# Two weight copies of a mixture-of-experts stage as a maximum, and three row-address steps moved up

## The reference

```python
x = x + xattn(norm(x), ctx, ctx, Wq, Wk, Wv, Wo, bo, mask)   # 16 heads of 64, causal
n = norm(x)
z = norm(n) * ln_g + ln_b
probs = softmax(z @ rW + rb)                                 # 8 experts
w = the two largest of probs, scaled to sum 1
hid[e] = gelu(z @ W1[e] + b1[e])                             # 128 -> 256
x = x + n + sum over e of w[e] * (hid[e] @ W2[e] + b2[e])    # 256 -> 128
```

## Time and profile before

| | |
|---|---|
| median of 3 runs | 913.03 us (911.52 to 915.53) |
| the profiled execution | 913.72 us, span of its instructions 912.0 us |
| PE, DVE busy in the span | 841.7 us, 736.0 us |
| ACT, POOL busy in the span | 607.7 us, 506.9 us |
| first and last tile's work | weights of tile 0 at 676.0 us, last scatter at 892.1 us |

### The profile page before, as it was taken

How to read it: one execution, slowest core, us unless ns; L and a number is a source line. 1 busy time by engine, 2 the same in 40 slices (tenths; PEclk the granted TensorE clock), 3 DMA queues, 4 the chain that set the end, 5 groups by cost and what they waited for, 6 DMA issues and landing times. The chain is left out here.

```text
span 912.0 us, 35805 instructions
## 1 busy us (share of the span) xinstructions
PE 841.7 (92%) x13368; PEld 740.8 (81%) x13368; DVE 736.0 (81%) x2243; ACT 607.7 (67%) x1317; POOL 506.9 (56%) x605
## 2 busy tenths in 40 slices
PE   8999899999999999999999999999989878888860
PEld 6989798888988898888988898988877767776750
DVE  5877689898988889898989998998867885656874
ACT  5676667776777767776677767786746644545763
POOL 3732545464645545464646545473455777777771
PEclk9999999999999999999999999999989999999995
DMA  9100101010010101010110101000103353336866
GB/s 298 51 25 3 43 9 41 6 41 23 29 35 12 38 9 41 6 41 14 39 32 15 38 9 41 6 29 9 46 18 88 100 136 97 101 99 172 238 194 219
DMA packets 55670, 56.72 MB, mean 62 GB/s; under 512 B 7335, under 2 KB 48593, under 8 KB 55601
## 3 DMA queue, kind: packets, MB, share of 16 engines
q1 hardware_dynamic: 46651, 37.94, 14.8%
q0 software_dynamic: 8640, 17.84, 5.8%
q10 hardware_dynamic: 310, 0.08, 0.0%
HBM read 32.62 MB, written 23.23 MB: 61 GB/s over the span
## 5 line engine op out<-in xcount | busy, mean ns | idle before, releaser
L901 PE MATMUL bank<-in_h,Ah 128*128 128x256 f32 x654 | 208.0, 318 | 16.7 <-DVE Al L1566 16.4
L771 ACT ACTIVATE pr<-pr 128x512 f32<-128x512 f32 x128 | 80.8, 631 | 183.8 <-DVE pr L1270 183.8
L700 POOL DMA_INDIRECT mixed<-kf,ix_i x142 | 144.3, 1016 | 50.2 <-issue 38.0
L724 ACT ACTIVATE kf<-bank 128x512 f32<-128x512 f32 x256 | 157.2, 614 | 2.1 <-PE bank L905 1.1
L905 PE MATMUL bank<-in_h,Al 128*128 128x256 f32 x512 | 144.7, 283 | 0.0
L902 PE MATMUL bank<-in_l,Ah 128*128 128x256 f32 x512 | 144.5, 282 | 0.0
L901 PEld LDWEIGHTS bank<-in_h,Ah 128*128 128x128 f32 x654 | 124.8, 191 | 24.0 <-DVE Al L1566 20.9
L605 POOL DMA_INDIRECT slots<-zrow,slot_ix x120 | 122.4, 1020 | 36.6 <-issue 22.7
L540 POOL TENSOR_TENSOR idle_p<-half 128x1 f32<-128x1 f32 x121 | 41.4, 345 | 167.0 <-DVE slot_ix L1361 144.7
L1016 PE MATMUL bank<-wo_s,oT 128*128 128x128 f32 x1024 | 133.1, 284 | 1.0 <-ACT oT L766 1.0
L1280 DVE TENSOR_TENSOR pr<-pr,ri 128x512 f32<-128x512 f32 x128 | 126.4, 988 | 4.4
(11 more groups left out here) (192 smaller groups left out, 1909.8 us busy)
## 6 DMA issues: line engine op xcount, KB each, us to landing
kf<-slots SPq DMA_DIRECT2D x71, 130.0 KB
kf<-mixed SPq DMA_DIRECT2D x12, 512.0 KB, 5.2
xs<-in_x_dram SPq DMA_DIRECT2D x16, 256.0 KB
c_in<-in_ctx_dram SPq DMA_DIRECT2D x16, 256.0 KB, 2.9
out_dram<-xs SPq DMA_DIRECT2D x16, 256.0 KB
mixed<-kf,ix_i POOLq DMA_INDIRECT x142
vf<-mixed SPq DMA_DIRECT2D x4, 512.0 KB, 4.1
slots<-zrow,slot_ix POOLq DMA_INDIRECT x120
```

The costliest lines, as they stand in the source:

```text
L700: pool.indirect_dma_start(out=mixed, out_offset=bass.IndirectOffsetOnAxis(ap=ix_i[buf][:, j:j + 1], axis=0), in_=y_sb[buf][:, j, :], in_of ...
L724: act.activation(kfs[par][:, 2 * u:2 * u + 2, :], ring[gr.bank(name)].rearrange("p (h t) -> p h t", h=2), ACT.Copy).then_inc(act_ev, 1)
L901: pe.matmul(ps, lh, rh, start=True, stop=False)
```

## The change

In `weights` the two larger copies become a maximum of the weights with themselves, which gives the same values: an operation with two inputs in place of one with one input. In `tile_in`, `places` of tiles 1, 2 and 3 moves from the tiles 4, 5 and 6, behind the `destinations` of its own tile. From tile 4 on the places stand where they stood.

```diff
-                dve.tensor_copy(w_r[deep], src[:, 0:2 * HF]).then_inc(wc_ok, 1)
-                dve.tensor_copy(w_f[deep], src[:, 2 * HF:2 * HF + B2]).then_inc(wc_ok, 1)
+                first, second = src[:, 0:2 * HF], src[:, 2 * HF:2 * HF + B2]
+                dve.tensor_tensor(w_r[deep], first, first, ALU.max).then_inc(wc_ok, 1)
+                dve.tensor_tensor(w_f[deep], second, second, ALU.max).then_inc(wc_ok, 1)
...
-                if s >= 4:
+                if s >= DEEP + 3:
                     places(s - 3, (k - 3) % DEEP)
                 if fresh:
                     weights(s + 1, (k + 1) % DEEP, e)
                 destinations(s + 1, (k + 1) % DEEP)
+                if s < DEEP - 1:
+                    places(s + 1, (k + 1) % DEEP)
```

## The result

The changed kernel takes 927.86 us (median of 5 runs, 927.42 to 930.54), the kernel before 913.73 us beside it (median of 5 runs, 911.52 to 915.53; three of them are those of the section on the time before). The ratio is 1.0153, with a 95% interval of 1.0132 to 1.0174: 14.1 us slower. The profiled execution took 927.86 us (span 926.1).

A forecast was written before the change was run, and what follows sets the result against it. Pace set by VectorE up to tile 16, GpSimd from 17 to about 50, then both to 67. Terms 6.0 + 6.5 + 2.2 = 14.7 us on 913.7 give 928.4, as a median 928 us; range 913 to 936.

The forecast's parts named there:

- Places of tiles 1 to 3: First tiles: tile 1 scattered 1.9 us earlier, but the gain covered by GpSimd's wait at tile 16: 0.
- Longer copies, up to tile 16: First tiles: maxima cost VectorE 0.36 us more in each of 18 tiles, less 0.5 us of waits: +6.0 us.
- hidden delay: Up to tile 16: rival, VectorE's delay is hidden while the meetings cost as forecast: 922 us, chance 0.06.
- The meetings in the middle tiles: Middle tiles: the first maximum holds GpSimd's second scatter 0.57 us, not 0.245, in 20 meetings: +6.5 us.
- The tiles with adds: Late tiles: 0.35 us more in each of 15 tiles, 3.1 us absorbed by waits for landings: +2.2 us.
- The sends: Eight GpSimd sends between tiles 16 and 17; the prediction gave them no term.
- both maxima holding: Middle tiles: rival, both maxima hold the scatter, 1.8 us scatters, term up to 14 us: 935 us, chance 0.12.
- the free port: All scatters: rival, a maximum leaves the port free, scatters all short: 914 us, no change, chance 0.15.

The follow-up runs named there:

- experiment 1: Only the places of tiles 1 to 3 moved, copies kept, against the kernel before: 914.95 us, ratio 0.999.
- experiment 4: The changed kernel with its first destination step rewritten as a scalar_tensor_tensor with three inputs: 924.28 us, ratio 1.0089 to the kernel before.
- experiment 3: The kernel before, copies kept, plus an unused VectorE reduction of 320 numbers in every tile: 924.64 us, ratio 1.0089.
- experiments 2 and 3: The first of the two: only the maxima, places kept, against the kernel before, 929.26 us, ratio 1.0152. The second has its own line.
- run 6: On the other chip, the kernel before with maxima for tiles 0 to 23 alone, copies from 24 on: 1029.36 us, ratio 1.0009.

## Why the prediction was right, and where it was wrong

- *Places of tiles 1 to 3, 0:* right, shown by experiment 1 (0.999).
- *Longer copies, up to tile 16, +6.0:* the direction, the place and the maxima's durations (0.69 and 0.42) were right, and the term was too small: it measured +8.1, and +8.3 with the maxima alone. What was missing is the destination step, which GpSimd's scatters stretch: 0.125 us in each of 18 tiles, or 2.3 us, and experiment 4 gives 2.7 for it. The rival's hidden delay isn't so: experiment 3's reduction moves tile 16 by 7.3 us.
- *The meetings in the middle tiles, +6.5:* **this is the step that failed**, and by its sign: -2.7 us. The size of a hold was nearly right (1.47 us, +0.51, predicted +0.57; the tile 3.03, predicted 3.08). The count was wrong: five meetings and not 20. I argued that VectorE has 0.9 us to spare against 0.36 more work. I left out two things: that VectorE must catch up with the landings after each late one, and that a running scatter stretches its destination step. After the late landing VectorE goes round in 2.53 us and GpSimd in 2.52, of which VectorE's own work is about 2.3. The stretched step takes up the rest, so VectorE never gets ahead. Experiment 3 shows the same without a maximum (no meetings, -5.6 us). Experiment 4 is the converse: with a short destination step VectorE waits for landings again (18.3 us in 30 tiles, against 7.3 us in 29 tiles of the changed kernel). Yet only nine scatters are held, where the changed kernel had six. A meeting also needs the maximum to start just ahead of a scatter, and there it mostly didn't. Why the landing at 782.9 was late is open. In the three kernels with maxima on every tile it is the same tile's address step that waits (tile 27: 2.98, 2.73 and 3.36 us), which speaks against chance.
- *The tiles with adds, +2.2:* mis-sized, +6.6. From the addresses of tile 48 to those of tile 67 lie the weights of 19 tiles, where I counted the 15 of a shorter stretch. Each costs 0.27 + 0.09 for the maxima and 0.17 for the destination step: 19 x 0.53 = 10.1 us (VectorE's busy time grew by 9.9). Its waits absorbed 5.6 of it and not the 3.1 that I named. The 2.3 us of lead that VectorE had lost in the middle, which I hadn't thought of, come on top.
- *The sends, not in the sum:* +2.0. I had costed them at nothing. GpSimd's queue is full there (0.30 us of issue before nearly every send), and VectorE runs operations of 1.10 us with two inputs beside them, which its delay moved closer to the start of the sends.
- *The rivals:* both maxima holding (1.8 us scatters) didn't occur, nor did the free port: the scatters at the meetings took 1.47 us. But what the free port stood for, a middle with short scatters, came about for the most part all the same, by timing.

So 928 was met because 9.2 us too many in the middle stood against 8.5 us too few in the three other stretches. That the total fits is luck. The direction isn't: the loss up to tile 16 and in the tiles with adds, which experiments 2 and 3 both have, makes the kernel slower whatever the middle does.

## What to carry to other kernels

Time added to an engine that has slack in one stretch isn't free if it sets the pace in another: read the price from each stretch, and count the tiles by the program's order. Where two engines meet in a cycle (a landing releases the one, whose work holds the other), cost the cycle only after asking what the engine must have to spare to come back to it after a slip; a longer operation can end the meetings as well as lengthen them. And when an operation is replaced, look at the untouched ones behind it, since they now start at another moment of the neighbour's work and can become longer by it.

## What the runs showed of the hardware

A maximum of 512 numbers with two inputs in SBUF does hold an indirect transfer of GpSimd that starts just behind it (1.47 for 0.96 us). One that starts 0.14 us behind the transfer doesn't hold it (experiment 4). The Trainium skill ("SBUF — State Buffer", Who interferes with whom) infers that `tensor_tensor` leaves descriptor generation alone; the trace of the changed kernel differs, and decides.

It goes the other way too. Of the 70 destination steps of the changed kernel, 2 numbers in a partition, 55 take 0.43 to 0.45 us in place of 0.21. They start 0.48 to 1.00 us behind the start of a scatter, whose own length is 0.95 to 1.47 us, and every one of them ends 0.03 to 0.05 us ahead of that scatter's end. Those that start within 0.34 us of a scatter's start keep their 0.21. In the kernel before one step of 70 is stretched. Written with three inputs the step stays at 0.20. In experiment 4 it has 0.20 us at 766.42, 1.00 us behind the start of a scatter of 1.47 us, and in the changed kernel it had 0.44 at 766.85, 0.99 us behind one of the same length:

```profile
766.42 0.20 DVE L1573 SCALAR_TENSOR_TENSOR kf<-kf,tile_code,half 128x2 f32<-128x2 f32 x1
```

```profile
766.85 0.44 DVE L1573 TENSOR_SCALAR kf<-kf,tile_code 128x2 f32<-128x2 f32 x1
```

The Trainium skill ("SBUF — State Buffer", Who interferes with whom) says that `tensor_scalar` can enter a mode that takes both ports, and that who issues first gets them for its whole instruction and the other waits. The trace agrees on the order (the step ends with the scatter); it doesn't show that a scatter blocks for its whole length, since steps near its start pass. The same section of the Trainium skill says that a reduction never contends on this chip, and with experiment 3's reduction the scatters had 960 ns, which agrees.

The kernel before took 913.0 us (three runs), 913.7 (these and two more) and 915.6 us (13 others), and 1036.1 and 1028.4 us in the two sets on the other chip. The mean granted clock was 0.978 in the one profiled execution and 0.947 in that of run 6 on the other chip. About half of the difference arises ahead of the tiles: the weights of tile 0 start at 676.0 us in the one and at 731.9 in the other, of spans of 912.0 and 1024.0. From 300 to 600 us the clock isn't the reason, as it was granted at 1.00, the higher of its two levels (2.4 GHz), on both (the kernel before and run 6). Part of what differs is a group of products that never waited and has 20.9 us of idle time in run 6 with no wait shown. The first row is the kernel before, the second run 6, both 100 to 600 us:

```profile
L1032 PE MATMUL bank<-kf 64*64 64x64 f32 x3136 | 58.3, 223 | 0.0
```

```profile
L1032 PE MATMUL bank<-kf 64*64 64x64 f32 x2856 | 73.6, 225 | 21.9 <-issue 20.9
```

What makes it so isn't settled here, and an edit worth 1.5% on the one chip showed nothing in its parts on the other.
